# An attention and FP4 feed-forward block: Silu on ScalarE, and one bucket of each of two sequences per tile

## The reference

```python
x = L0_attn_x                                   # (8, 2048, 256)
xn = layernorm(x)
q, k, v = split(xn @ W_qkv.T)                   # 16 heads of 16
q = softmax(q) * HEAD_DIM ** -0.5;  k = exp(k)
b_q, b_k, b_v = bucket(q), bucket(k), bucket(v) # buckets of 64 tokens
context  = shifted_cumsum(einsum('bhnsd,bhnse->bhnde', b_k, b_v))
k_cumsum = shifted_cumsum(sum(b_k, -2))         # both: sums over the buckets before
den  = einsum('bhnsd,bhnd->bhns', b_q, k_cumsum)
attn = einsum('bhnsd,bhnde,bhns->bhnse', b_q, context, 1 / max(den, 1e-6))
a = attn @ W_out.T

gate = fp4_linear(xn, w_gate)                   # 704 columns, blocks of 16
y    = fp4_linear(xn, w_up)
f = fp4_linear(silu(gate) * y, w_down)          # quantises its input and the weight
return x + a + f
```

## Time and profile before

| | |
|---|---|
| median of 3 runs | 1790.64 us (1788.91 to 1790.73) |
| the profiled execution | 1790.21 us, span of its instructions 1788.5 us |
| VectorE busy | 1723.7 us, 96% of the span |
| TensorE busy | 1677.6 us, 94% |
| ScalarE busy | 1142.6 us, 64% |
| GpSimd busy | 599.4 us, 34% |
| TensorE clock granted | 0.988 of full speed on average |
| DMA | 37.01 MB, 21 GB/s over the span |

### The profile page before, as it was taken

One profiled execution on the slowest core, in us unless ns is written; L12 is line 12 of the kernel. 1 busy time (PEld: TensorE's weight loads), 2 busy tenths in 40 slices (PEclk: granted clock), 3 DMA queues, 4 the chain that ended last, 5 costly groups with the idle time before them and its releaser, 6 DMA issues.

```text
span 1788.5 us, 47623 instructions
## 1 busy us (share of the span) xinstructions
PE 1677.6 (94%) x12366; PEld 1147.8 (64%) x12366; DVE 1723.7 (96%) x4655; ACT 1142.6 (64%) x2840; POOL 599.4 (34%) x1053
## 2 busy tenths in 40 slices
PE   0289999999999999999999999999999999999997
PEld 0256666666666666666666666666666666666665
DVE  6769999999999999999999999999999999999997
ACT  2756666666666666666666666666666666666663
POOL 2723232333333333333333333333333333333330
PEclk9889999999999999999999999999999999999998
DMA  3000000000000000000000000000000000000000
GB/s 101 1 0 13 23 23 18 18 23 23 12 23 23 12 23 23 21 14 23 23 12 23 23 17 18 23 23 12 23 23 12 23 23 23 12 23 23 12 12 19
DMA packets 35849, 37.01 MB, mean 21 GB/s; under 512 B 2118, under 2 KB 35142, under 8 KB 35654
## 3 DMA queue, kind: packets, MB, share of 16 engines
q1 hardware_dynamic: 35830, 36.77, 6.7%
HBM read 19.99 MB, written 16.78 MB: 21 GB/s over the span
## 4 chain that ended last, share of the span: by engine, by line
DVE 44%; issue 32%; PE 11%; ACT 6%; DVEq 4%; POOL 2%; DMA 1%; ACTq 1%; SPq 0%; POOLq 0%
DVE hq_s L832 7%; DVE dmx L707 4%; DVE ga L727 4%; DVE hv L798 3%; DVE qmax L671 3%; DVE h L737 2%; DVE xq_s L845 2%; DVE drec L711 1%; ACT hqt L552 1%; ACT th L542 1%; DVE qsh L680 1%; DVE osum L868 1%; DVE xq_s L843 1%; ACT qexp L484 1%; DVE dz L703 1%
## 5 line engine op out<-in xcount | busy, mean ns | idle before, releaser
L348 POOL TENSOR_TENSOR xnt<-xnt 128x256 f16<-128x256 f32 x128 | 118.7, 928 | 728.1 <-ACT xnt L466 728.1
L552 ACT ACTIVATE hqt<-trp 128x512 f16<-128x512 f16 (+1 forms) x384 | 213.5, 556 | 183.1 <-PE trp L1108 180.8
L1127 PE MATMUL outp<-w_down_cat,hqt 128*128 128x256 f16 x1408 | 247.3, 274 | 0.0
L525 ACT ACTIVATE hm<-hv 128x704 bf16<-128x704 f32 x128 | 101.0, 789 | 153.9 <-DVE hv L798 153.9
L744 DVE TENSOR_REDUCE hblk<-h 128x44 f32<-128x704 f32 x128 | 183.9, 1436 | 0.1
L1050 PE MATMUL ctxp<-vaug,kexp 64*128 64x136 f32 x996 | 181.4, 302 | 0.0
L1041 PE MATMUL nump<-snap,qt 128*64 128x144 f32 x1024 | 180.8, 299 | 0.4 <-DVE snap L691 0.4
L502 ACT ACTIVATE att_t<-trp 128x256 f32<-128x256 f32 x128 | 49.2, 384 | 194.9 <-PE trp L1062 194.8
L1050 PEld LDWEIGHTS ctxp<-vaug,kexp 64*128 64x128 f32 x996 | 131.2, 186 | 49.5 <-issue 49.1
L339 POOL TENSOR_TENSOR att_t<-att_t 128x256 f16<-128x256 f32 x128 | 86.2, 673 | 218.1 <-ACT att_t L503 218.1
L355 POOL TENSOR_TENSOR xmid<-xmg,xv 128x256 f32<-128x256 f32 x128 | 117.0, 914 | 108.3 <-ACT xmg L517 108.3
(11 more groups left out here) (219 smaller groups left out, 5157.5 us busy)
## 6 DMA issues: line engine op xcount, KB each, us to landing
xring<-x SPq DMA_DIRECT2D x64, 256.0 KB, 2.7
out<-xring SPq DMA_DIRECT2D x64, 256.0 KB, 2.2
raw_qkv<-wqkv_t SPq DMA_DIRECT2D x1, 768.0 KB, 13.6
raw_gate<-wgate SPq DMA_DIRECT2D x1, 704.0 KB
raw_up<-wup SPq DMA_DIRECT2D x1, 704.0 KB
raw_down<-wdown SPq DMA_DIRECT2D x1, 704.0 KB, 12.2
raw_out<-wout_t SPq DMA_DIRECT2D x1, 256.0 KB, 13.4
```

The source lines that it names most:

```text
L348: nc.gpsimd.tensor_tensor(xnt[:, par, 1, :], xnt32[:, par, :], xnt[:, par, 0, :], ALU.subtract)\
L552: nc.scalar.activation(hqt[:, par, m0:m1, :], tr16[:, 0:(m1 - m0) * P] .rearrange("p (m k) -> p m k", k=P), ACT.Copy).then_inc(hqt_done, 1)
L1127: nc.tensor.matmul(downp, hqt[:, par, m, :], w_down_cat[:, m, :], start=(m == 0), stop=False)
```

## The change

Three things change together.

Silu: ScalarE evaluates Silu of the gate instead of tanh (`silu_gate`), and VectorE multiplies the result with the up half from PSUM in one instruction (`gate_h`). The instruction `ga` and its semaphore go. Two scale factors are adapted.

Tiles: rows 0 to 63 of a tile are a bucket of one sequence, rows 64 to 127 the bucket of the same number of the next sequence. There are 32 tiles per pair of sequences, still 128 in all. Both buckets need sums that end with the tile before, so there is one snapshot per tile and one call of `bucket`. Four `nump` matmuls give 64 rows each, alternating between the upper and the lower half of the output rows; four `ctxp` matmuls contract over all 128 rows, with the values of each sequence in columns of their own and zeros in the other's rows, and alternate between output rows 0 to 63 and 64 to 127. The copy of the values becomes two copies of 64 rows. Each load and store of x becomes two DMAs, one per half of the partitions.

Memory: `hq_s` and `hqt` lie in the buffer `q_rows`, which is free after the start. In the orders below they are therefore called q_rows.

```diff
-                nc.scalar.activation(vaug[:, par, :, 0:P], kv[:, D:2 * D].rearrange("p (g e) -> p g e", g=HG), ACT.Copy,
-                                     scale=2.0 ** -19).then_inc(kv_done, 1)
+                for s in range(2):
+                    rows = slice(s * BUCKET, (s + 1) * BUCKET)
+                    nc.scalar.activation(vaug[rows, par, :, :, s, 0:VW].rearrange("p g f e -> p (g f) e"),
+                                         kv[rows, D:2 * D].rearrange("p (o e) -> p o e", e=VW), ACT.Copy,
+                                         scale=2.0 ** -19).then_inc(kv_done, 1)
...
-                nc.scalar.activation(th[:, half, :], unit[(par + half) % 2][0][:, 0:FH], ACT.Tanh, scale=c_g[:, :])\
-                    .then_inc(tanh_done, 1)
+                nc.scalar.activation(sg[:, half, :], unit[(par + half) % 2][0][:, 0:FH], ACT.Silu, scale=c_g[:, :])\
+                    .then_inc(silu_done, 1)
...
-                nc.vector.tensor_tensor(snap[:, b, :, 0:CW], ctxp[:, 0:HG * CW].rearrange("p (g c) -> p g c", g=HG),
-                                        mask[:, 0:CW].rearrange("p (o c) -> p o c", o=1).broadcast_to([P, HG, CW]),
-                                        ALU.mult).then_inc(snap_done, 1)
+                sums = ctxp[:, 0:2 * HG * CW].rearrange("p (i o c) -> p i o c", o=1, c=CW).broadcast_to([P, 2 * HG, 2, CW])
+                nc.vector.tensor_tensor(snap[:, :, :, :, 0:CW].rearrange("p g s f c -> p (g s) f c"), sums,
+                                        mask[:, :, :].rearrange("p (o f) c -> p o f c", o=1)
+                                        .broadcast_to([P, 2 * HG, 2, CW]), ALU.mult).then_inc(snap_done, 1)
...
-                nc.vector.scalar_tensor_tensor(ga[:, half, :], th[:, half, :], 1.0,
-                                               unit[(par + half) % 2][0][:, 0:FH], ALU.add, ALU.mult)\
-                    .then_inc(ga_done, 1)
...
-                nc.vector.tensor_tensor(h[:, par, half * FH:(half + 1) * FH], ga[:, half, :],
+                nc.vector.tensor_tensor(h[:, par, half * FH:(half + 1) * FH], sg[:, half, :],
                                         unit[(par + half) % 2][1][:, 0:FH], ALU.mult).then_inc(h_done, 1)
...
-                snapshot(k, 1)
...
                 gate_h(k, 0, par)
                 row_factor(k - 1, odd)
-                times_up(k, 0, par)
...
-                snapshot(k + 1, 0)
+                snapshot(k + 1)
                 attention(k, par, 2)
                 gate_h(k, 1, par)
                 attention(k, par, 3)
-                times_up(k, 1, par)
...
                 for g in range(HG):
-                    last = nc.tensor.matmul(nump[rows, g * SW:(g + 1) * SW],
-                                            qt[:, par, g * P + b * BUCKET:g * P + (b + 1) * BUCKET],
-                                            snap[:, b, g, :], start=True, stop=True)
+                    for s in range(2):
+                        rows = slice(s * BUCKET, (s + 1) * BUCKET)
+                        last = nc.tensor.matmul(nump[rows, g * 2 * SW:(g + 1) * 2 * SW],
+                                                qt[:, par, g * P + s * BUCKET:g * P + (s + 1) * BUCKET],
+                                                snap[:, g, s, :, :].rearrange("p f c -> p (f c)"), start=True, stop=True)
...
                 for g in range(HG):
-                    last = nc.tensor.matmul(ctxp[:, g * CW:(g + 1) * CW], kexp[rows, par, g * P:(g + 1) * P],
-                                            vaug[rows, par, g, :], start=False, stop=False, skip_group_check=True)
+                    for f in range(2):
+                        last = nc.tensor.matmul(ctxp[f * VW:(f + 1) * VW, g * 2 * CW:(g + 1) * 2 * CW],
+                                                kexp[:, par, g * P + f * VW:g * P + (f + 1) * VW],
+                                                vaug[:, par, g, f, :, :].rearrange("p s c -> p (s c)"),
+                                                start=False, stop=False, skip_group_check=True)
...
-                bucket(k, 0, par, False)
+                bucket(k, par, ends)
                 gate_up(k, 0, par, (0,))
                 transpose_h(k - 2, par, 1)
                 gate_up(k, 0, par, (1,))
                 transpose_h(k - 2, par, 2)
-                bucket(k, 1, par, ends)
                 gate_up(k, 1, par, (0,))
```

More of the change, by code:

```diff
@@ L154, in linear_attention_fp4_ffn_block @@
         hq = sb("hq", [P, F], bf16)
-        hq_s = sb("hq_s", [P, 2, 2 * F], fp16)
-        hqt = sb("hqt", [P, 2, HT, P], fp16)
+        hq_s = q_flat[:, 0:4 * F].rearrange("p (t k) -> p t k", t=2)
+        hqt = q_flat[:, 4 * F:4 * F + 2 * HT * P].rearrange("p (t m k) -> p t m k", t=2, k=P)
         osum = sb("osum", [P, 2, D])
@@ new lines, in _, with load, store @@
+            halves = [slice(s * BUCKET, (s + 1) * BUCKET) for s in range(2)]
+            def load(q, n):
+                i = q * SP_N + n
+                if not isinstance(i, int) or i >= 1:
+                    sp.wait_ge(x_in, i * 32)
+                if not isinstance(i, int) or i >= XCH:
+                    sp.wait_ge(x_out, (i - XCH + 1) * 32)
+                for s in range(2):
+                    sp.dma_start(xring[halves[s], n % XCH, :, :], x_dram[q, n, s]).then_inc(x_in, 16)
+            def store(q, n):
+                i = q * SP_N + n
+                if not isinstance(i, int) or i >= 1:
+                    sp.wait_ge(x_out, i * 32)
+                sp.wait_ge(o_step, (i + 1) * 4)
+                for s in range(2):
+                    sp.dma_start(out_dram[q, n, s], xring[halves[s], n % XCH, :, :]).then_inc(x_out, 16)
@@ L273, in _ @@
             for n in range(XCH):
-                load(n)
+                load(0, n)
                 if n >= STORE_LAG:
-                    store(n - STORE_LAG)
-            with sp.Fori(XCH, NP) as n:
-                load(n)
-                store(n - STORE_LAG)
-            for n in range(NP - STORE_LAG, NP):
-                store(n)
-            sp.wait_ge(x_out, NP * 16)
+                    store(0, n - STORE_LAG)
+            with sp.Fori(XCH, SP_N) as n:
+                load(0, n)
+                store(0, n - STORE_LAG)
@@ L285, in _ @@
+            with sp.Fori(1, NT // SEQ_TILES) as q:
+                for n in range(STORE_LAG):
+                    load(q, n)
+                    store(q - 1, SP_N - STORE_LAG + n)
+                with sp.Fori(STORE_LAG, SP_N) as n:
+                    load(q, n)
+                    store(q, n - STORE_LAG)
+            for n in range(SP_N - STORE_LAG, SP_N):
+                store(NT // SEQ_TILES - 1, n)
+            sp.wait_ge(x_out, NP * 32)
         @block.gpsimd
@@ L305, in _ @@
                                         pattern=[[-step, n] for step, n in pat], channel_multiplier=-1).then_inc(pool_zero, 1)
-            pool.wait_ge(pool_zero, 15)
+            pool.wait_ge(pool_zero, 13)
             nc.gpsimd.tensor_copy(ident16[:, :], ident32[:, :]).then_inc(consts, 1)
-            for b in range(2):
-                for g in range(HG):
-                    nc.gpsimd.tensor_copy(snap[:, b, g, CW:SW], mask[:, CW:SW]).then_inc(consts, 1)
+            for s in range(2):
+                pool.wait_ge(consts, 1 + s)
+                nc.gpsimd.memset(vaug[s * BUCKET:(s + 1) * BUCKET, :, :, :, s, VW:CW], 1.0).then_inc(consts, 1)
+            pool.wait_ge(consts, 3)
+            for g in range(HG):
+                for s in range(2):
+                    nc.gpsimd.tensor_copy(snap[:, g, s, :, CW:SW], mask[:, :, VW:CW]).then_inc(consts, 1)
             pool.wait_ge(w_max, 6)
@@ L534, in copy_xqt, with silu_gate @@
                     .then_inc(xqt_done, 1)
-            def tanh_gate(t, half, par):
+            def silu_gate(t, half, par):
                 if not is_tile(t):
@@ L977, in _ @@
         def _(pe):
-            pe.wait_ge(consts, 5)
+            pe.wait_ge(consts, 7)
             def clear_context():
-                nc.tensor.matmul(ctxp[:, 0:HG * CW], zeros16[:, 0:P], zeros16[:, :], start=True, stop=True,
+                nc.tensor.matmul(ctxp[:, 0:2 * HG * CW], zeros16[:, 0:P], zeros16[:, :], start=True, stop=True,
                                  skip_group_check=True).then_inc(ctx_done, 1)
@@ L1030, in transpose_q, with bucket @@
                 last.then_inc(qt_tr, 1)
-            def bucket(t, b, par, clears):
+            def bucket(t, par, clears):
                 if not is_tile(t):
                     return
-                rows = slice(b * BUCKET, (b + 1) * BUCKET)
-                pe.wait_ge(snap_done, after(t, 2, b + 1))
+                pe.wait_ge(snap_done, after(t))
                 pe.wait_ge(qt_done, after(t))
@@ L1085, in gate_up @@
                     pe.wait_ge(q_shift, after(t + 1))
-                    pe.wait_ge(kv_done, after(t + 1, 2))
+                    pe.wait_ge(kv_done, after(t + 1, 3))
                 cols = slice(half * FH, (half + 1) * FH)
```

113 lines of the change are left out of this document (50 added, 63 removed).

## The result

| | before | after |
|---|---|---|
| median of 4 runs, same chip | 1790.0 us (1788.91 to 1790.73) | 1857.0 us (1856.64 to 1858.47) |
| ratio to before, 95% interval | | 1.0378 [1.0361, 1.0394] |
| predicted | | 1860, range 1805 to 1935 |

A forecast was written before the change was run, and what follows sets the result against it. VectorE sets the old pace of 13.1 us; then a ring through ScalarE's table loads does. Ring A gives 1884, ring B 1835; the middle, 0.54 a tile, gives 1790.2 + 69 = 1859, rounded to 1860, range 1805 to 1935.

The forecast's parts named there:

- the waits at qexp, hmid and h: TensorE waits 1.5 us or more at qexp for xnt; VectorE waits at hmid for hm and at h for sg.
- ring B: TensorE's qexp load via att_t, ScalarE's queue with both table loads, back to qexp, no bucket: 13.45 us, 0.35 over.
- The reasoning on the load: Each ScalarE table load takes 1.28 us and cannot overlap its neighbours, so 1.38 each, ends 1.28 and 1.5.
- the bucket block: TensorE's nump and ctxp matmuls put together: 2.1 us, at best 1.05 if the array's halves run side by side.
- ring A: TensorE's qexp load through the bucket, ScalarE's queue with one table load, back to qexp: 13.83 us, 0.73 over old pace.
- The upper end of the range: Ring A with 0.2 more at each load, 14.2 us a tile: 1935 us.
- VectorE's floor: VectorE's own work per tile falls by 0.9, from 13.1 to 12.2 us, through fewer ga and snapshot instructions.
- Rival 1: Both table loads hide in ScalarE's idle time between att_t and Silu: pace 12.6, 1726 us; chance 9%.
- Rival 2: Each ScalarE table switch costs another 1.28 us beside the load: ring B 16.0, 2161 us; chance 5%.
- Rival 3: No change: the loads eat exactly what the engines win, rings at 13.05 to 13.15, 1790 us; chance 3%.
- The DMAs: Each load and store becomes two of 128 KB; covered by the buffer ring, they cost nothing, otherwise 2.7 us each at most.

The follow-up runs named there:

- the kernel with the early load: The changed kernel plus a tiny 128x1 exp on ScalarE ahead of the att copies, moving one table load into its wait: 1756.84 us, ratio 0.9817.
- the run without loads: The changed kernel with tanh evaluated where it evaluates Silu, nothing else changed: 1611.85 us, ratio 0.9009 to the kernel before.

## Why the prediction was right

**The mechanism.** The prediction held that the sums of all engines fall and that a ring through ScalarE's two table loads takes over. It does: no engine above 85%, the waits at qexp, hmid and h where they were foretold, 253 loads, a pace of 13.65 within 13.4 to 13.9. Taking the loads out gives 1611.9, taking one link out of ring B 1791.7, and taking that link out with the load moved gives nothing.

**Which ring.** This was left open between A and B with half the chance each, and the runs say B alone. Its links by the prediction and in the rows of after:

| link of ring B | predicted | measured |
|---|---|---|
| qexp (911.27) to att_t (917.27) | 6.00 | 6.00 |
| att_t to kexp, load included | 0.55 + 1.38 | 1.97 |
| kexp | 0.36 | 0.38 |
| two copies of the values | 0.66 | 0.79 |
| hqt, hm, hqt | 1.56 | 1.54 |
| qexp to sg, load included | 0.40 + 1.38 | 1.82 |
| sg, xnt, to qexp | 1.16 | 1.16 |
| sum | 13.45 | 13.66 |

**The size that was off in B** is 0.21: the copies cost 0.13 more, the two loads 0.04 more each, and the plain links nothing (0.02 more and 0.02 less). The reasoning on the load held. It takes 1.28, but it starts only when the instruction before has ended, so the overlap of 0.1 is lost as well: from qexp to the first gate instruction it is 1.82 with a load and 0.40 without, 1.42 for the load where 1.38 was taken. The copies were priced "like the one before" at 0.33, which is the 0.40 of the old copy less an overlap; no row before shows an instruction close behind that copy. In a queue without waits one copy moves the next start by 0.26 and two by 0.79. The first of the two still overlaps kexp, the second starts 0.02 after the first has ended, and q_rows 0.02 after the second. So the second is worth 0.53, not 0.33. At 128 tiles this is 68 us; the run with one copy gained 65, nearly the whole loss.

**The step that failed** is the bucket block in ring A, 2.1. It is 1.10, by the lower end of the bounds (1.05), and the halves of the array do run side by side. The Trainium skill, "TensorE: Matmul & The Clock Gate", the part on packing small matmuls, says so of three narrower column groups, and I had let it change no chance; the trace agrees, 0.44 for eight rows on two halves and for four on one. With 1.10 ring A is 11.64 + 1.38 - 0.19 = 12.83 by the prediction's own links, and the kernel with the early load, where A is the longest ring, measures 12.80. So the links of A were right and only this term was wrong, by 1.0 us. (The refill in it is the second of three, not the first.)

**Why the number was right.** 1860 was the middle between an A that was too long by 1.0 and a B that was too short by 0.2. B by its measured links gives 1790.2 + 128 x (13.65 - 13.1) = 1861. The middle hit it by luck; a reader should trust the links of B and not the mean. The upper end of the range was also too wide by its own terms: it adds 0.2 to each of two loads, and ring A passes one, so 13.83 + 0.2 and 1909.

**VectorE's floor** was put at 12.2. The window gives 347.46 / 400 x 13.65 = 11.86, and the run without loads has a pace of 11.7 with VectorE full. The two ga instructions were counted right: of the 12.2, the run without loads lacks one meeting with GpSimd, the product of hq and hs_lo at 519 ns instead of the 1053 before, and 12.2 less 0.53 is its 11.7. What was missing is that VectorE's meetings with GpSimd lie elsewhere in each kernel, here in the changed kernel, over 1000 us:

```profile
L811 DVE SCALAR_TENSOR_TENSOR hv<-h,hblk 128x704 f32<-128x704 f32 x73 | 78.7, 1078 | 0.0
...
L730 DVE SCALAR_TENSOR_TENSOR dmx<-dz 128x16 f32<-128x16 f32 x74 | 12.1, 163 | 0.0
```

dmx takes 163 ns, against 694 with the tiles alone, while hv grew from 0.88 to 1.08. The snapshot of 544 elements takes 0.71, predicted 0.69. None of this reached the time, since VectorE is off the path.

**The rivals.** Rival 1, the loads hide, needed ring A with the short block, which came, and a ring B 0.35 shorter, which did not. Rival 2, a switch that costs twice the load: in ScalarE's rows above qexp ends at 922.46, the load goes from 922.48 to 923.76, and the Silu begins at 923.77. That is 0.02 before it and 0.01 behind it. The 1283 ns of the Trainium skill, "ScalarE: Activation LUTs", "What ACT_TABLE_LOAD costs", agree to the nanosecond; its 1380 ns of drain do not show in this queue, where a load adds 1.42 from start to start and not 2.66, and the measurement decides. Rival 3, no change, is what the kernel with one copy of the values measures (1791.7). The DMAs land in 2.6 us in twice as many pieces and nothing waits for them.

## What to carry to other kernels

Where every engine is well filled, add up the rings and not only the engines: follow one instruction from engine to engine back to itself, and write down its slack. A ring with 0.0 slack bills each added instruction in full, and two edits that are each nearly free (+7 and -8 us here) can cost 67 together when both put something into the same ring. A switch of ScalarE's table set is one instruction of 1.28 us, worth 1.42 in a queue without waits, that stands where the compiler finds the next function of the other set: a tiny activation of that set, put where ScalarE waits anyway, moves it there. Here this and one reorder in TensorE turned 3.8% slower into 5.3% faster.

## What the runs showed of the hardware

- Float32 matmuls with 64 output rows that go to the upper and the lower half of the array's output run side by side: eight weight loads take 0.44 us, as four on one half do. They need not alternate in the queue (block 1.15 against 1.10 when all of one half come first), and a matmul for one half can start before an earlier one for the other (902.19 against 902.31).
- A table load takes 1.28 us in ScalarE's queue, starts 0.02 after the instruction before has ended and is followed after 0.01. With the lost overlap it adds 1.42 from start to start. A longer emptying of the engine does not show.
- Work of GpSimd lengthens an instruction of VectorE by up to 0.54 us (518 to 1055 ns for the product of hq and hs_lo), even one of 128 x 16 elements (163 to 694 ns) and one of 128 x 44 (247 to 646 ns), and where this falls changes with each change of timing. So a VectorE time read from one kernel does not hold for its variant to better than some 0.5 us a tile.
- A copy of 64 partitions takes as long as one of 128 (0.77 for two against 0.38 for one). In a queue without waits the pair costs more than double, 0.79 against 0.26 from start to start, since the second copy, on partitions 64 to 127, overlaps neither neighbour. Whether the number of partitions or the change of the first one does this was not tried.
